# A sequence-convolution and expert kernel on one core: half of the x blocks and the columns of kernel numbers turned by VectorE instead of TensorE

## What is computed

```python
u_m = u * mask[:, None, :]
K = 2.0 * jnp.einsum('hn,hnl->hl', Cs, jnp.exp(P)).real
y = jnp.fft.irfft(jnp.fft.rfft(u_m, n=n) * jnp.fft.rfft(K, n=n), n=n)[..., :Lq]
y = (y + u_m * D[:, None]) * mask[:, None, :]
logits = jnp.einsum('bsd,ed->bse', y, route_w)
topk_v, topk_idx = jax.lax.top_k(logits, 1)
route_weight = jax.nn.one_hot(topk_idx[..., 0], E) * topk_v
h = jnp.einsum('bsd,erd->bser', y, A)
out = x + jnp.einsum('bser,eor->bso', route_weight[..., None] * h, Bw)
```

## Time and profile before

| | |
|---|---|
| median of 3 runs (616.24 to 616.44) | 616.39 us |
| the profiled execution, its own time | 616.44 us |
| its span in the trace | 614.6 us |
| TensorE busy | 587.9 us (96%) |
| VectorE busy | 481.1 us (78%) |
| GpSimd busy | 385.9 us (63%) |
| ScalarE busy | 327.5 us (53%) |
| TensorE clock granted | full in all 40 slices |
| DMA packets, bytes | 37071, 77.65 MB |

### The profile page before, as it was taken

The page is one execution under the profiler, slowest core; times in us unless marked ns, Lnnn a source line. Parts: engine busy times, 40 slices in busy tenths (PEclk is TensorE's granted clock), DMA queues, the critical chain, the costliest instruction groups (busy, mean ns, idle before and its releaser), DMA issues.

```text
span 614.6 us, 13508 instructions
## 1 busy us (share of the span) xinstructions
PE 587.9 (96%) x3681; PEld 532.4 (87%) x3681; DVE 481.1 (78%) x1305; ACT 327.5 (53%) x1123; POOL 385.9 (63%) x520
## 2 busy tenths in 40 slices
PE   3579999999999999999999999999999999999996
PEld 3468899899989989998998999999899999989984
DVE  7678778787877878787787888777777877777875
ACT  3677664556456455545645554564555456455420
POOL 4667756666675666667566667757566775665430
PEclk9999999999999999999999999999999999999999
DMA  6113344345344434433443453454454344344422
GB/s 128 63 53 100 135 153 137 106 147 154 96 138 155 125 115 149 153 97 139 154 115 125 149 149 100 141 155 112 125 152 142 103 144 155 102 134 153 132 85 86
DMA packets 37071, 77.65 MB, mean 126 GB/s; under 512 B 11836, under 2 KB 20350, under 8 KB 36998
## 3 DMA queue, kind: packets, MB, share of 16 engines
q1 hardware_dynamic: 27846, 43.76, 28.0%
q10 hardware_dynamic: 9152, 33.03, 13.2%
HBM read 43.16 MB, written 33.62 MB: 125 GB/s over the span
## 4 chain that ended last, share of the span: by engine, by line
PE 92%; DVE 4%; ACT 2%; issue 1%; POOL 1%; DMA 0%; ACTq 0%; POOLq 0%; DVEq 0%
PE psYo L1062 19%; PE psZ L1084 19%; PE psO L1062 15%; PE psYe L1062 13%; PE psS L1062 11%; PE psO L1111 5%; PE psXe L1073 4%; PE psXo L1073 4%; PE psZ L1150 1%; PE psS L1123 1%; DVE psS L931 0%; DVE ex L773 0%; DMA logs<-in_L_cond_log_dt_dram 0%; POOL both L469 0%; DVE ost L963 0%
## 5 line engine op out<-in xcount | busy, mean ns | idle before, releaser
L508 POOL TENSOR_TENSOR Slo<-Sf,Shi 128x384 fp32r<-128x384 f32 x64 | 65.4, 1021 | 172.5 <-ACT Shi L661 172.5
L931 DVE SCALAR_TENSOR_TENSOR psS<-Sf,tab,psS 64x128 f32<-64x128 f32 x256 | 91.9, 359 | 50.2 <-ACT Sf L656 42.7
L1084 PE MATMUL psZ<-Wt,Y 128*128 128x136 f32 x1024 | 129.2, 279 | 0.0
L1084 PEld LDWEIGHTS psZ<-Wt,Y 128*128 128x128 f32 x1024 | 123.3, 190 | 0.1
L656 ACT ACTIVATE Sf<-psS 128x128 f32<-128x128 f32 x64 | 17.8, 277 | 193.1 <-PE psS L1062 192.9
L963 DVE TENSOR_TENSOR ost<-psO,xt 128x512 f32<-128x512 f32 x128 | 88.4, 691 | 1.7 <-PE psO L1062 1.1
L501 POOL TENSOR_TENSOR Xlo<-xeven,Xhi 128x512 fp32r<-128x512 f32 x64 | 82.4, 1287 | 0.0
L469 POOL TENSOR_TENSOR both<-coarse,fine 128x512 f32<-128x512 f32 x64 | 68.8, 1075 | 1.3 <-ACT fine L595 1.2
L947 DVE TENSOR_TENSOR wlo<-psZ,whi 128x128 fp32r<-128x128 f32 x64 | 18.7, 292 | 55.5 <-ACT whi L666 55.5
L1062 PE MATMUL psO<-Bw_hi,whi 128*128 128x512 f32 x128 | 50.4, 394 | 0.7 <-ACT whi L666 0.7
L1062 PE MATMUL psYo<-Xlo,Thi 128*128 128x512 f32 x128 | 50.8, 397 | 0.0
(11 more groups left out here) (197 smaller groups left out, 1541.4 us busy)
## 6 DMA issues: line engine op xcount, KB each, us to landing
xt<-in_x_dram SPq DMA_DIRECT2D x64, 512.0 KB, 4.9
out_dram<-ost ACTq DMA_DIRECT2D x63, 512.0 KB, 5.2
Traw<-kdram SPq DMA_DIRECT2D x64, 128.0 KB, 2.9
kdram<-krow SPq DMA_DIRECT2D x64, 1.0 KB
A_nat<-in_L_ffn_A_dram SPq DMA_DIRECT2D x1, 512.0 KB, 5.1
B_nat<-in_L_ffn_Bw_dram SPq DMA_DIRECT2D x8, 64.0 KB, 3.5
out_dram<-ost SPq DMA_DIRECT2D x2, 256.0 KB, 2.0
lens_i<-in_itok_B_dram SPq DMA_DIRECT2D x1, 64.0 KB, 4.2
```

The source lines that it names most:

```text
L508: pool.tensor_tensor(Slo[h.s2][:, :], Sf[h.s2][:, :], Shi[h.s2][:, :].bitcast(F32), ALU.subtract).then_inc(slo_done, 1)
L931: dve.scalar_tensor_tensor(psS[to, new], Sf[h.s2][fr, old], tab2[fr, BR, h.n:h.n + 1], psS[to, new], ALU.mult, ALU.add).then_inc(brought_d ...
L1084: last = pe.matmul(psZ[:, 0:NW], Y[:, j, c, :], Wt[:, 2 * c + j, :], start=(j == 0 and c == 0), stop=(j == 1 and c == NE - 1), skip_group_ ...
```

## The change

The odd blocks of x are no longer turned by TensorE. They are loaded a second time from HBM, in 16 pieces for each head. A piece (g, c) holds the 32 positions g of odd block c, for all 128 batches, and lands on 32 partitions of a new tile `xblk` (two of them in turn), as 128 runs of 32 numbers, 128 bytes each. With this layout one 32 x 32 block transpose of the whole tile on VectorE (`turn_blocks`, 128 x 512) gives the same matrix `xodd` that TensorE's four transposes gave in `psXo`, in SBUF instead of PSUM. In a loop step SyncE issues 11 of the 16 pieces, right behind the load of x, and ScalarE issues 5, ahead of everything else in its step.

With it: the odd half is rounded by ScalarE out of `xodd` (`x_hi_odd`, now right behind `first_state`), its rest is taken by GpSimd (`x_lo_odd`, ahead of `s_lo`) and no longer by VectorE. VectorE turns the blocks at the head of its step, ahead of `carry`.

The two columns of kernel numbers `kcol` get room for 32 numbers each, with zeros in the rest, and VectorE turns them (`turn_k`, 128 x 64, ahead of `b_lo`) straight into `krow`. TensorE's transpose and ScalarE's `k_row` go. `skew_kernel` moves from the end of SyncE's step to the head of the next one, where it stands ahead of `load_x`. At the start of the program, 16 pieces for each of the heads 0, 1 and 2 are added (head 0's on both queues: 8 ahead of the loads of `B_nat` on SyncE and 8 at the very head of ScalarE), and the transposes of the second table now stand ahead of those of `B_nat` on TensorE.

```diff
+        xblk = [sb(f"xblk{s}", [P, NE, G4, G32]) for s in range(2)]
+        xodd = sb("xodd", [P, HALF])
...
-        kcol = [sb(f"kcol{s}", [P, 2]) for s in range(2)]
-        krow = [sb(f"krow{s}", [2, P]) for s in range(2)]
+        kcol = [sb(f"kcol{s}", [P, 2, G32]) for s in range(2)]
+        krow = [sb(f"krow{s}", [P, 2, G32]) for s in range(2)]
...
+        PIECES = [(g, c) for g in range(G4) for c in range(NE)]
+
+        def load_blocks(eng, h, pieces):
+
+            need(eng, xodd_done, h.n - 1)
+            for g, c in pieces:
+                eng.dma_start(xblk[h.s2][g * G32:(g + 1) * G32, c, :, :],
+                              bass.AP(x.tensor, h.n * L + c * Q + P + g * G32,
+                                      [[H * L, G32], [G32 * H * L, G4], [1, G32]])
+                              ).then_inc(blk_in[h.s2], 16)
+
...
+                need(sp, k_turned, h.n + 1)
-                sp.dma_start(bass.AP(kdram.tensor, h.s2 * (P + Q), [[P, 2], [1, P]]),
-                             krow[h.s2][:, :]).then_inc(k_out[h.s2], 16)
+                sp.dma_start(bass.AP(kdram.tensor, h.s2 * (P + Q), [[G32, P // G32], [P, 2], [1, G32]]),
+                             krow[h.s2][0:P:G32, :, :]).then_inc(k_out[h.s2], 16)
...
             def step(head):
+                if head(1).there and not is_head(head(0), 1):
+                    skew_kernel(head(1))
                 if head(2).there:
                     load_x(head(2))
+                    load_blocks(sp, head(2), PIECES[:11])
                     write_kernel(head(2))
-                    skew_kernel(head(2))
 
             load_x(Head(0))
...
+            load_blocks(sp, Head(0), PIECES[:8])
...
+            load_blocks(sp, Head(1), PIECES)
...
+                if n == 1:
+                    load_blocks(sp, Head(2), PIECES)
...
+            def x_lo_odd(h):
+
+                need(pool, xhi_odd, h.n + 1)
+                need(pool, y_mm, (h.n - 1) * 2)
+                pool.tensor_tensor(Xlo[h.s2][:, 1, :], xodd[:, :], Xhi[h.s2][:, 1, :].bitcast(F32),
+                                   ALU.subtract).then_inc(xlo_odd, 1)
+
...
                 if head(3).there and not is_head(head(0), 1):
                     g_table(head(3))
+                if head(1).there:
+                    x_lo_odd(head(1))
                 if head(0).there:
                     s_lo(head(0))
...
+            load_blocks(act, Head(0), PIECES[8:])
+            act.wait_ge(cols_set, 4)
...
-            def k_row(h):
-
-                need(act, k_turned, h.n + 1)
-                need(act, k_out[h.s2], h.half * 16)
-                act.activation(krow[h.s2][:, :], psK(h), ACT.Copy).then_inc(krow_done, 1)
...
+            def x_hi_even(h):
+                need(act, xt_done, h.n + 1)
                 need(act, y_mm, (h.n - 1) * 2)
-                act.activation(eo(Xhi[h.s2], j), psX[j][:, :], ACT.Copy).then_inc(xhi_done, 1)
+                act.activation(eo(Xhi[h.s2], 0), psX[0][:, :], ACT.Copy).then_inc(xhi_even, 1)
+
+            def x_hi_odd(h):
+                need(act, xodd_done, h.n + 1)
+                need(act, y_mm, (h.n - 1) * 2)
+                act.activation(eo(Xhi[h.s2], 1), xodd[:, :], ACT.Copy).then_inc(xhi_odd, 1)
...
+                if head(2).there:
+                    load_blocks(act, head(2), PIECES[11:])
                 if head(-2).there:
                     store(head(-2))
                 if head(0).there:
                     first_state(head(0))
+                if head(1).there:
+                    x_hi_odd(head(1))
                 if head(3).there:
                     m_matrix(head(3))
                 if head(1).there:
-                    x_hi(head(1), 0)
-                    x_hi(head(1), 1)
+                    x_hi_even(head(1))
                 if head(2).there:
                     b_hi(head(2))
...
-                if head(2).there:
-                    k_row(head(2))
...
+            def turn_blocks(h):
+
+                need(dve, blk_in[h.s2], (h.half + 1) * 16 * G4 * NE)
+                need(dve, xlo_odd, h.n)
+                dve.transpose(xodd[:, :], xblk[h.s2][:, :, :, :].rearrange("p c g i -> p (c g i)")
+                              ).then_inc(xodd_done, 1)
...
+            def turn_k(h):
+
+                need(dve, kcol_done, h.n * 2 + 2)
+                need(dve, k_out[h.s2], h.half * 16)
+                dve.transpose(krow[h.s2][:, :, :].rearrange("p j w -> p (j w)"),
+                              kcol[h.s2][:, :, :].rearrange("p j w -> p (j w)")).then_inc(k_turned, 1)
...
+                if head(1).there:
+                    turn_blocks(head(1))
                 if head(0).there:
                     carry(head(0))
-                if head(1).there:
-                    x_lo(head(1))
...
                 if head(2).there:
+                    turn_k(head(2))
                     b_lo(head(2))
...
-            def turn_x(h, j):
+            def turn_x(h):
-                need(pe, *((xlo_odd, h.n) if j else (xeven_done, h.n)))
+                need(pe, xeven_done, h.n)
                 for c in range(NE):
-                    at = (2 * c + j) * P
-                    last = pe.transpose(psX[j][:, c * P:(c + 1) * P], xt[h.s4][:, at:at + P], ident[:, :])
+                    at = 2 * c * P
+                    last = pe.transpose(psX[0][:, c * P:(c + 1) * P], xt[h.s4][:, at:at + P], ident[:, :])
                 last.then_inc(xt_done, 1)
...
+                need(pe, xhi_even, h.n + 1)
+                need(pe, xhi_odd, h.n + 1)
...
-                if h.n > 1:
-                    need(pe, krow_done, min(h.n + 2, H))
+                if is_head(h, 0):
+                    pe.wait_ge(w_done, 3)
...
-            def turn_k(h):
-
-                need(pe, kcol_done, h.n * 2 + 2)
-                need(pe, krow_done, h.n)
-                if h.n < 3:
-                    pe.wait_ge(w_done, 3)
-                else:
-                    need(pe, s_carried, (h.n - 1) * 2)
-                pe.transpose(psK(h), kcol[h.s2][:, :], ident[:, :]).then_inc(k_turned, 1)
...
```

68 lines of the change are left out of this document (27 added, 41 removed).

## The result

The changed kernel takes 636.58 us (median of 4 runs, 635.3 to 637.85), the kernel before 616.41 (4 runs beside it): a ratio of 1.033, interval 1.031 to 1.035. The prediction of 589 us, its range and its sign were wrong. The profiled execution has a span of 635.2 us where before had 614.6.

What follows compares the result with a forecast made beforehand. TensorE was taken to bound the loop at 8.99 us a step; 614.6 - 34.0 + 5 (stalls) + 1 (start) = 586.6 us of span, 588.4 with 1.8 around it, forecast 589 us, range 581 to 611 us.

Steps and rivals of the forecast that it cites:

- What bounds the kernel, and what TensorE gets back: TensorE's own work sets the loop step; without its transposes a step goes from 8.99 to 8.44 us, 34.0 us in all.
- SyncE's queue: Behind the load of x, 11 issues of 0.33 us, 3.6 us; last piece issued at s + 3.4, landed in time.
- Rival 2: SyncE issues pieces slowly: at 0.58 us, 11 take 6.4 us, no gain, 612 to 617 us; chance 0.06.
- Rival 3: DMA engines become the bound: slower than before above 40 ns a packet, 697 us at 50 ns; chance 0.15 with slower otherwise.
- VectorE's transpose: Ahead of `carry`: 0.61 us; fits plain steps, `carry` 0.44 us late with `frac`, stalling TensorE 0.14 us once in four steps.
- the spare of 0.85 us: Between the end of `Slo` and TensorE's want of it in the kernel before; 0.30 us left in the changed kernel.
- the clamp's trouble with `whole`: `whole` on VectorE took 1.33 us beside GpSimd, otherwise 0.22; a rival had the transpose wait likewise, up to 612 us.
- `whi`: ScalarE's `whi` is 0.55 us late in the step with `mirror`, stalling 0.20 us; just covered with `turns`.
- the spare of 0.35 us: Between the end of `whi` with its signal and `up` on TensorE, set against `whi` coming 0.55 us late.
- The five issues ahead of `store`: ScalarE's five piece issues, 1.7 us, covered by its wait of 3.24 us for `bring`.
- The second subtraction: GpSimd's `x_lo_odd` ahead of `Slo`, 1.28 us, fits by 0.1 us; costed at nothing, 8 us in all without cover.
- The start: Eight pieces ahead of `B_nat` on SyncE and ScalarE's five issues in step 1: +1 us, bounds -1 and +3.

Runs made afterwards that it cites:

- e6_fewer: Changed kernel with SyncE's pieces one head earlier and the row's write ahead of its last three, 6 of those 11 pieces left out from the fifth head on: 606.05 us.
- e10_gap_fewer: e6_fewer with VectorE's transpose moved behind `b_lo`, and the transpose and ScalarE's pieces one head further on: 605.7 us (2 runs).
- e12_whi: e11_start with `whi` ahead of `turns` and `mirror` on ScalarE: 598.9 us, ratio to the kernel before 0.973.
- e5_k_only: Kernel before with only the kernel numbers turned by VectorE (`turn_k`), x as before and no pieces: 609.06 us, ratio 0.989.
- e7_thin: e6_fewer with all 16 issues of a head kept, but each with 32 of its 128 runs from the fifth head on: 610.58 us.
- e4_traffic: Kernel before with all 16 pieces of each head loaded but never read, and the skewed read at the head of SyncE's step: 630.47 us (1 run).
- e11_start: e10_gap_fewer with all pieces loaded, and those of the third and fourth heads spread over gaps in SyncE's queue at the start: 610.83 us, ratio 0.990.

## Why the prediction was wrong, point by point

**What bounds the kernel, and what TensorE gets back: right.** A step without other waits takes 8.42 to 8.43 us (e6_fewer, e10_gap_fewer, e12_whi) where 8.44 was forecast, and `turn_k` alone brought 7.3 us where 61 x 0.11 = 6.7 were.

**SyncE's queue: the step that failed.** The prediction put eleven pieces at 3.6 us, the last at s + 3.4, and went on: "The skewed read moved into the next step is then issued as soon as the write has landed." It priced what the moved instruction does and not what its wait does. Four terms were mis-sized or missing. The issue: 0.33 us was taken from the load of x, which stands alone in its queue; a piece takes 0.43 us and 0.04 to the next, and some take 0.7 us and more (up to 3.1), so 6.0 us in place of 3.6. The issue of x itself: 0.58 us in the mean, for 0.33. The write's issue: 0.24 us became 0.54 now that it gathers eight runs of 128 bytes from four partitions; e5_k_only, without pieces, has the same 0.54. And the landing: before, SyncE waited 52.4 / 62 = 0.85 us for it each step, hidden because the queue then stood idle for several microseconds until `krow` was there; in the changed kernel the skewed read stands at the head of the step, with x and the pieces of the next head behind it, and the wait had grown to 1.5 us. All of it lies in one row: 0.35 + 0.58 + 6.0 + 0.54 + 1.5 + 0.3 for the gaps = 9.3 us. The row of waits was there in the trace of before and I didn't read it, since its engine was idle most of the time.

The Trainium skill ("DMA: Bandwidth & Descriptors", Anatomy of one DMA) has this as a rule, though told of GpSimd's path: most of a small transfer's fixed cost is the receipt from the target memory, HBM above all, and a wait on it stands on the issuing sequencer. The trace agrees that a wait on a small write can cost SyncE's queue more than its issue: 1 KB to HBM held it for 0.85 us and, with the pieces about, for 1.5. That the receipt is what takes this time no run here shows.

**Rival 2 named the place and not the mechanism.** It had the issues at 0.58 us and 6.4 us for eleven, near what came (6.0), and deduced no gain at worst. What it lacked is again the landing, with which SyncE's row is longer than TensorE's 8.99 us before, so that a loss and not only a lost gain follows.

**Rival 3, the DMA engines: wrong as priced, right in kind for a little.** The DMA share times the step was 0.43 x 8.99 = 3.9 us and is 0.59 x 9.27 = 5.5: 1.6 us more a step, where 1.7 was forecast from 13 ns a packet. Nothing was near full. Yet neighbours slow down: the skewed read lands after 4.3 us in the median instead of 2.9, and with three quarters of the runs left out the step was 0.12 us shorter (e7_thin). (The load's "about 150 GB/s" should have been 173, from 133 x 8.99 us and 262 KB in 8.44 us; no chance hung on it. e12_whi moved 165.)

**VectorE's transpose: size right, place mis-sized.** It takes 0.70 us and `carry` starts 0.73 after it, where 0.61 was taken. But the step with `frac` lost 0.6 us and not 0.14, and three terms made it so. "0.75 us by their spacing" was 0.94, since the clamp took 0.63 us beside GpSimd's `Grev` (308.70 to 309.45) and 0.23 in the kernel before. With the transpose's 0.12 that makes `carry` 0.75 us late where 0.44 was forecast. And the spare of 0.85 us was read at the weight load of `Slo` (307.37), but TensorE waits for `Slo` ahead of the load of `Shi`, 0.11 us earlier, so 0.19 us were left and not 0.30: 0.75 - 0.19 = 0.56, near the 0.6 measured. The row of the kernel before:

```profile
307.26 0.19 PEld L1062 LDWEIGHTS psYe<-Shi,Ghi 128*128 128x128 f32 x1
```

The prediction had seen the clamp's trouble with `whole` and had looked for it at the transpose alone. By the Trainium skill ("SBUF — State Buffer", Who interferes with whom) VectorE in a two-port mode and GpSimd shut one another out of a shared pair of ports for a whole instruction; the trace agrees in that the clamp is 0.40 us longer beside `Grev` and ends only behind it, by 0.08 us, and the transpose kept 697 to 714 ns throughout.

**ScalarE: `whi` mis-sized.** 0.20 us in one step of four was forecast, "just covered" for `turns`; measured were 0.42 (8.85 against 8.43) and 0.26 (8.69). The failed term is the spare of 0.35 us, counted from the end of `whi`. `up` waits for `wlo` too, and in the kernel before `wlo` ended at 326.14 in the step with `mirror`, 0.09 us ahead of the load that wants it (326.23): 0.55 - 0.09 = 0.46. These and the clamp make 8.74 of 8.43, 19 us in all where 5 were forecast. e12_whi, with `whi` ahead of both, got 0.17 us a step of this back by order alone. The five issues ahead of `store` were covered while they were five.

**GpSimd: right.** The second subtraction, 1.28 us, didn't show in any chain that I read.

**The start: mis-sized.** +1 us with bounds to +3 was forecast; the third `Sf` came 4.3 us late. The third head's 16 pieces go out behind the second skewed read in 7.7 us, the first `carry` of the loop waits for the transpose of them, and TensorE for `wh`; then its clock is down for a while. After, in order of time and by windows:

```profile
44.96 0.71 DVE L920 STREAM_TRANSPOSE xodd<-xblk 128x512 f32<-128x512 f32 x1 [4.88 <-DMA xblk<-in_x_dram]
```

```profile
49.25 0.38 PE L1180 MATMUL psZ<-ident,wh 128*128 128x128 f32 x1 [3.51 <-DVE wh L949]
```

```profile
49.00:53.00 4.00, 3.64 (x11) 3.20 (x12) 2.33 (x6) 1.73 (x8) 3.92 (x5) 0.57 0.18 28
```

Before, TensorE waited 1.24 us at this place and kept a clock of 1.00 in the same four microseconds. I had counted ScalarE's issues and the eight pieces ahead of `B_nat`, and not these 16.

**What stays open.** Why single issues of a piece last 1 to 3 us when most last 0.43; whether it is the queue's depth or the engines behind it was not separated. How the loss of e4_traffic comes about step by step. And whether e11_start's earlier start stands in all its runs.
